# First attention's queries and keys in 256 natural columns, with the mask added by products on TensorE

## What is computed

```python
q = _split_heads(query @ Wq.T + bq)      # query: layernorm(x)
k = _split_heads(key @ Wk.T + bk)        # key, value: the context
v = _split_heads(value @ Wv.T + bv)
scores = jnp.einsum('bhqd,bhkd->bhqk', q, k) / SCALE
scores = jnp.where(attn_mask == 0, jnp.float32(-1000000000.0), scores)
w = jax.nn.softmax(scores, axis=-1)
att = jnp.einsum('bhqk,bhkd->bhqd', w, v)
x = att + key                             # then a layernorm with gamma, beta
```

## Time and profile before

| | us |
|---|---|
| median of three runs | 1006.89 |
| profiled execution | 1014.34 |
| its span, first to last instruction | 1012.5 |
| TensorE busy in the span | 912.5 |
| VectorE busy | 619.8 |
| ScalarE busy | 478.3 |
| GpSimd busy | 351.2 |
| first scores (L576) start | 20.4 |
| last scores (L576) start | 183.3 |

### The profile page before, as it was taken

One profiled execution on the slowest core, in us unless ns is written; L12 is line 12 of the kernel. 1 busy time (PEld: TensorE's weight loads), 2 busy tenths in 40 slices (PEclk: granted clock), 3 DMA queues, 4 the chain that ended last, 5 costly groups with the idle time before them and its releaser, 6 DMA issues. The chain is left out here.

```text
span 1012.5 us, 27004 instructions
## 1 busy us (share of the span) xinstructions
PE 912.5 (90%) x9232; PEld 785.4 (78%) x9233; DVE 619.8 (61%) x1609; ACT 478.3 (47%) x1241; POOL 351.2 (35%) x506
## 2 busy tenths in 40 slices
PE   5899999877999999998999899999999998659996
PEld 4788888637899999986474788888888887547784
DVE  3588888654455555542026556867668668249995
ACT  2878878612222222222344444444444443249894
POOL 1245545430000000007002554555545453246662
PEclk9999999888999999999999989999999999879997
DMA  4454456346811111116854999898897977211221
GB/s 139 143 162 148 151 171 203 121 162 208 298 47 47 47 52 45 48 37 215 308 208 140 170 187 178 147 193 167 175 189 150 203 161 133 47 38 55 63 65 42
DMA packets 220908, 138.34 MB, mean 137 GB/s; under 512 B 159648, under 2 KB 206240, under 8 KB 220704
## 3 DMA queue, kind: packets, MB, share of 16 engines
q1 hardware_dynamic: 173392, 90.86, 36.7%
q10 hardware_dynamic: 44368, 38.08, 13.7%
q0 software_dynamic: 3072, 8.39, 2.7%
HBM read 82.31 MB, written 54.98 MB: 136 GB/s over the span
## 5 line engine op out<-in xcount | busy, mean ns | idle before, releaser
L1604 ACT ACTIVATE c_pT<-c_T 128x512 f32<-128x512 f32 (+2 forms) x90 | 50.2, 595 | 103.6 <-PE c_T L1760 71.8
L1557 POOL TENSOR_TENSOR c_soft<-c_soft,c_share 128x616 f32<-128x616 f32 (+2 forms) x96 | 70.4, 761 | 62.5 <-DVE c_share L2013 60.8
L1027 ACT ACTIVATE b_rowsT<-b_RT 128x256 f32<-128x256 f32 x39 | 15.0, 386 | 161.1 <-PE b_RT L1075 161.1
L1144 DVE COPY b_w<-moe_w 128x1024 f32 x78 | 53.6, 689 | 54.7 <-issue 51.4
L1532 POOL COPY c_pick<-tile_rows 128x2 int32<-128x2 int32 (+1 forms) x16 | 2.9, 179 | 229.7 <-POOLq L934 229.7
L1084 PEld LDWEIGHTS b_G<-b_rowsT,b_w 128*128 128x128 f32 x624 | 77.2, 195 | 4.3 <-DVE b_w L1144 1.5
L1084 PE MATMUL b_G<-b_rowsT,b_w 128*128 128x128 f32 x624 | 77.9, 279 | 1.5 <-ACT b_rowsT L1027 1.3
L1158 DVE SCALAR_TENSOR_TENSOR b_hidT<-b_U,b_bias,b_gate 128x128 f32<-128x128 f32 x156 | 43.9, 344 | 56.6 <-PE b_U L1084 50.4
L1084 PE MATMUL b_U<-b_rowsT,b_w 128*128 128x128 f32 x624 | 76.0, 275 | 0.0
L1111 PE MATMUL b_Y<-moe_w,b_hidT 128*128 x312 | 73.9, 380 | 0.9 <-DVE b_out L1188 0.9
L1084 PEld LDWEIGHTS b_U<-b_rowsT,b_w 128*128 128x128 f32 x624 | 72.8, 192 | 0.0
(11 more groups left out here) (230 smaller groups left out, 2172.3 us busy)
## 6 DMA issues: line engine op xcount, KB each, us to landing
rel_windows<-c_relw ACTq DMA_DIRECT2D x28, 368.0 KB
c_bias<-rel_windows SPq DMA_DIRECT2D x16, 616.0 KB, 5.0
prob_rows<-c_soft SPq DMA_DIRECT2D x16, 616.0 KB
moe_w<-in_L_Wl SPq DMA_DIRECT2D x16, 512.0 KB
values<-c_pT ACTq DMA_DIRECT2D x22, 256.0 KB, 2.6
b_rows<-expert_lists SPq DMA_DIRECT2D x39, 128.0 KB, 2.0
expert_out<-b_out SPq DMA_DIRECT2D x39, 128.0 KB
c_v<-values SPq DMA_DIRECT2D x16, 308.0 KB
```

What stands on the lines that cost most here:

```text
L1144: nc.vector.tensor_copy(own[p][h][:, :, :], w1[:, bass.ds(e, 1), :, h * HE:(h + 1) * HE].rearrange("p o c n -> p (o c) n"))\
L1557: ins = nc.gpsimd.tensor_tensor(soft[p][:, hs, a:z], soft[p][:, hs, a:z], share[:, s, hs].unsqueeze(2).to_broadcast([P, HS, z - a]), ALU.mult)
L1604: nc.scalar.activation(dst, view(T[k]), ACT.Copy, **kw).then_inc(g["emptied"], 1)
```

## The change

The weights of queries and keys keep their 256 columns, two tiles c of 128. A strip of 32 rows now holds two heads. The keys are written twice, kT[:, c, u, :], with the rows of the other head zeroed (keep now has two sides u); one product of a strip's queries (both heads, 32 rows) with both copies (256 columns) gives the scores of both heads. The mask is no longer carried in column 16: four products ahead of the scores, one for each strip, add -1e9 to masked positions. They multiply ones by a tile of 16-bit floats (bf16), masked, whose three nonzero rows hold parts of -1e9 that bf16 holds exactly. keep and masked are computed on GpSimd, three tensor_scalar instructions for each batch, two steps ahead, between std(0) and std(1) of a step; VectorE's keep_mask goes. The wait of load(b + 4) on keep stays as written, though keep is now counted a step later. ScalarE evicts two query tiles instead of four; VectorE writes the keys by two instructions of 256 columns instead of four of 128. In attend the probabilities are picked from other banks (strip, side). As the tiles' addresses shift, two waits for copies out are added in experts.

```diff
@@ layer0, tiles
-        wq = sb("a_wq", [P, KD, MT0 * P])
-        wk = sb("a_wk", [P, KD, MT0 * P])
+        wq = sb("a_wq", [P, KD, D])
+        wk = sb("a_wk", [P, KD, D])
-        keep = [sb(f"a_keep{p}", [P, P]) for p in range(2)]
+        keep = [sb(f"a_keep{p}", [P, 2, P]) for p in range(2)]
+        masked = [sb(f"a_masked{p}", [P, P], BF16) for p in range(2)]
+        ones_b = sb("a_ones", [P, P], BF16)
-        qT = sb("a_qT", [P, MT0, P])
-        kT = sb("a_kT", [P, MT0, P])
+        qT = sb("a_qT", [P, KD, P])
+        kT = sb("a_kT", [P, KD, 2, P])
@@ GpSimd
+            def masks(b, p):
+                if not isinstance(b, int) or b > 1:
+                    apart(pool, g["s_mm"], b - 1)
+                for u in range(2):
+                    nc.gpsimd.tensor_scalar(keep[p][:, u, :], mask_in[p][:, :], 0.0, cst("side")[:, u:u + 1], ALU.is_equal, ALU.is_lt)
+                nc.gpsimd.tensor_scalar(masked[p][:, :], mask_in[p][:, :], 0.0, cst("masked"), ALU.is_equal, ALU.mult)\
+                    .then_inc(g["keep"], 1)
...
-            for b in range(3):
+            for b in range(2):
                 std(0, b)
+                masks(b, b)
+            std(0, 2)
...
             def steps(b, i, p):
                 if there(b + 3):
                     std(0, b + 3)
+                if there(b + 2):
+                    masks(b + 2, p)
                 if there(b - 2):
                     std(1, b - 2)
                     std(2, b - 2)
@@ ScalarE, queries
-                for m in range(MT0):
+                for m in range(KD):
@@ TensorE
-                strips(M[0], wq, [xT[p][:, c, :] for c in range(KD)], range(MT0), g["q_mm"])
+                strips(M[0], wq, [xT[p][:, c, :] for c in range(KD)], range(KD), g["q_mm"])
-                strips(M[1], wk, [cT[p][:, c, :] for c in range(KD)], range(MT0), g["k_mm"])
+                strips(M[1], wk, [cT[p][:, c, :] for c in range(KD)], range(KD), g["k_mm"])
...
-            def scores(b):
+            def scores(b, p):
+                strip = [slice(j * STRIP, (j + 1) * STRIP) for j in range(HPT)]
+                pe.wait_ge(g["keep"], b + 1)
+                since(pe, g["s_exp"], 2 * b)
+                for j, r in enumerate(strip):
+                    nc.tensor.matmul(S[j][:, :, :], ones_b[r, :], masked[p][r, :].unsqueeze(1).to_broadcast([STRIP, MT0, P]),
+                                     start=True, stop=False)
                 pe.wait_ge(g["q_sb"], b + 1)
                 pe.wait_ge(g["k_sb"], b + 1)
-                since(pe, g["s_exp"], 2 * b)
-                for m in range(MT0):
-                    for j in range(HPT):
-                        r = slice(j * STRIP, (j + 1) * STRIP)
-                        ins = nc.tensor.matmul(S[j][:, m, :], qT[r, m, :], kT[r, m, :], start=True, stop=True)
+                for c in range(KD):
+                    for j, r in enumerate(strip):
+                        ins = nc.tensor.matmul(S[j][:, 2 * c:2 * c + 2, :], qT[r, c, :], kT[r, c, :, :], start=False, stop=(c == KD - 1))
                 ins.then_inc(g["s_mm"], 1)
@@ VectorE
-            def keep_mask(b, p):
-                since(dve, g["k_sb"], b - 1)
-                nc.vector.tensor_scalar(keep[p][:, :], mask_in[p][:, :], 0.0, cst("aug"), ALU.not_equal, ALU.not_equal)\
-                    .then_inc(g["keep"], 1)
...
-                for m in range(MT0):
-                    ins = nc.vector.scalar_tensor_tensor(kT[:, m, :], M[1][:, m * P:(m + 1) * P], bk[:, m:m + 1],
-                                                         keep[p][:, :], ALU.add, ALU.mult)
+                for c in range(KD):
+                    ins = nc.vector.scalar_tensor_tensor(kT[:, c, :, :], M[1][:, c * P:(c + 1) * P].unsqueeze(1).to_broadcast([P, 2, P]),
+                                                         bk[:, c:c + 1], keep[p][:, :, :], ALU.add, ALU.mult)
...
-                if front:
-                    keep_mask(b + 3, 1 - p)
@@ experts
+            for out in shared["s_text_out"]:
+                pool.wait_ge(out, 16 * EARLY_HALVES // TEXT_BANKS)
             nc.gpsimd.memset(zeros[:, :], 0.0).then_inc(s_zero, 1)
...
-            dve.wait_ge(shared["s_text_out"][2], 16 * EARLY_HALVES // TEXT_BANKS)
+            for out_copy in shared["s_text_out"][2:]:
+                dve.wait_ge(out_copy, 16 * EARLY_HALVES // TEXT_BANKS)
             combine()
```

More of the change, by code:

```diff
@@ L39 @@
 SCALE0 = 1.0 / DH0 ** 0.5
-MASKED = -1.0e9
+MASKED_PARTS = (-998244352.0, -1753088.0, -2560.0)
+assert sum(MASKED_PARTS) == -1.0e9
 EPS0 = 1e-6
@@ L106, in constants @@
     c["halves"] = np.concatenate([np.eye(P // 2, dtype=np.float32)] * 2)
-    aug = np.zeros((P, 1), np.float32)
-    aug[DH0::STRIP] = 1.0
-    c["aug"] = aug
+    row = np.arange(P)
+    c["side"] = np.stack([row % STRIP // DH0 == u for u in range(2)], axis=1).astype(np.float32)
+    parts = np.zeros((P, 1), np.float32)
+    for n, part in enumerate(MASKED_PARTS):
+        parts[n::STRIP] = part
+    c["masked"] = parts
     e = np.arange(NE, dtype=np.float32)
@@ L161, in layer0 @@
         ident, before, ones = cst("ident"), cst("before"), cst("ones")
-        wq = sb("a_wq", [P, KD, MT0 * P])
-        wk = sb("a_wk", [P, KD, MT0 * P])
+        wq = sb("a_wq", [P, KD, D])
+        wk = sb("a_wk", [P, KD, D])
         wv = sb("a_wv", [P, KD, D])
         wr = sb("a_wr", [P, KD, NE])
-        bq = sb("a_bq", [P, MT0])
-        bqs = sb("a_bqs", [P, MT0])
-        bk = sb("a_bk", [P, MT0])
+        bq = sb("a_bq", [P, KD])
+        bqs = sb("a_bqs", [P, KD])
+        bk = sb("a_bk", [P, KD])
         bv = sb("a_bv", [P, D])
@@ L382, in _ @@
                 nc.gpsimd.memset(va[p][:, :, :], 1.0).then_inc(s_setup, 1)
-            pool.wait_ge(s_setup, 4)
+            nc.gpsimd.memset(ones_b[:, :], 1.0).then_inc(s_setup, 1)
+            pool.wait_ge(s_setup, 5)
+            pool.wait_ge(s_const, 16)
             def inverse_std(link, eps, ready, done, b, k):
@@ L437, in _ @@
             act.wait_ge(s_bqs, 1)
-            act.wait_ge(s_setup, 4)
+            act.wait_ge(s_setup, 5)
             def project(b, p):
@@ L597, in attend @@
                     for k in range(HPT):
+                        strip, side = 2 * (m % 2) + k // 2, 2 * (m // 2) + k % 2
                         ins = nc.tensor.matmul(T[0][k * STRIP:(k + 1) * STRIP, m * P:(m + 1) * P], va[p][:, m * HPT + k, :],
-                                               pT[k][:, m, :], start=True, stop=True, tile_position=(0, k * STRIP))
+                                               pT[strip][:, side, :], start=True, stop=True, tile_position=(0, k * STRIP))
                 ins.then_inc(g["pv_mm"], 1)
@@ L651, in steps @@
                 if there(b):
-                    scores(b)
+                    scores(b, p)
                 if there(b - 1):
@@ L715, in norm_in @@
                 norm_var(norm_stats(b, i, p))
-                keep_mask(b, p)
                 norm_rows(b, p)
@@ L2595, in layout @@
         "x": x, "ctx": ctx_1024, "mask": mask_Bx1x1xS2_ik0.reshape(NB, P),
-        "L0_wqT": strip_columns(L0_xattn_Wq), "L0_wkT": strip_columns(L0_xattn_Wk), "L0_wvT": c(L0_xattn_Wv.T),
+        "L0_wqT": c(L0_xattn_Wq.T), "L0_wkT": c(L0_xattn_Wk.T), "L0_wvT": c(L0_xattn_Wv.T),
         "L0_wrT": c(L0_ffn_Wr.T),
-        "L0_bq": strip_bias(L0_xattn_bq, 1.0 / SCALE0), "L0_bk": strip_bias(L0_xattn_bk, MASKED), "L0_bv": L0_xattn_bv,
+        "L0_bq": L0_xattn_bq.reshape(KD, P).T, "L0_bk": L0_xattn_bk.reshape(KD, P).T, "L0_bv": L0_xattn_bv,
         "L0_gamma": L0_xattn_gamma, "L0_beta": L0_xattn_beta, "L0_br": L0_ffn_br, "L0_pick_bias": L0_ffn_biases_N,
```

9 lines of the change are left out of this document (removed).

## The result

| | before | after |
|---|---|---|
| median of the runs, us | 1007.21 (1006.24 to 1011.64) | 1019.68 (1018.1 to 1020.2) |
| span of the profiled execution, us | 1012.5 | 1017.6 |
| granted clock, mean of the span | 0.967 | 0.954 |
| mean of six loop steps, L765 / L784 to the next, us | 11.34 | 13.06 |

A forecast was written before the change was run, and what follows sets the result against it. The prediction took a ring through GpSimd and VectorE, 10.86 us in a step of 11.55, as the bound, with TensorE's ring close behind. Terms: 1006.89 + 9.6 at full clock + 6.0 for the clock = 1022.5 us; range 1004 to 1036.

The forecast's parts named there:

- the ring: GpSimd scatters, std(0), std(1), VectorE's rows_scaled, keys, list counts, slots, next scatter: 10.86 us, said to hold the loop step.
- M: Time of GpSimd's three mask instructions between std(0) and std(1): 0.70 us each plus 0.05 wait, 2.15 us.
- start and steps up to 3: Start -4.0 us from fewer weights and records; steps 0 and 1 -0.8; steps 2 and 3 +1.8.
- three static steps: The three steps before the loop, where std(1) likewise follows std(0): 3 x 1.4 = +4.2 us.
- six loop steps, full clock: Rolled loop of the first attention: 12.76 us a step instead of 11.34, +8.5 us in all.
- the step after: The step behind the loop, without std(0): 11.4 us instead of 10.46, +0.9.
- last four steps: End of the first attention, where masks have ended: -1.0 us.
- from there to the experts: Stretch between the last attention steps and the experts' first transposes: no term was given.
- clock in the long steps: TensorE's clock halves in idle gaps: 1.5 us a step, expected in 4 of 10 long steps, +6 us.
- rivals D and B: D: price and gains cancel, M near 1.35, 1005 to 1009 us, chance 0.07. B: cheap masks, about 1002, chance 0.13.
- Rival A: Gaps don't bring TensorE's clock down, the ring still costs: 1016.5 us, chance 0.25.
- SyncE: load(b + 4) waits for the masks, leaving some 6 us later in the step: costs nothing, over 3 us to spare.

The follow-up runs named there:

- filling the gap: Changed kernel plus six unused TensorE products ahead of the transposes that wait for the keys, from step 3 on; ratio 1.0082 to the kernel before.
- loads apart: Changed kernel, masks between std(1) and std(2), x's load no longer waiting for keep, mask's load last with its own semaphore; ratio 1.0018 to the kernel before.

## Why the prediction held, and where it didn't

Direction, size and place held: 1022.5 forecast, 1019.68 measured, through the ring that was named. Term by term:

| term | forecast | measured |
|---|---|---|
| one mask set, M | 2.15 | 2.39 |
| start and steps up to 3 | -3.0 | -2.8 |
| three static steps | +4.2 | +4.3 |
| six loop steps, full clock | +8.5 | +10.3 with its falls |
| the step after | +0.9 | +0.8 |
| last four steps | -1.0 | -3.4 |
| from there to the experts | 0 | +2.2 |
| clock in the long steps | +6 | about +2 to +3, within the rows above |
| whole | +15.6 | +12.5 by the medians, 6.8 to 14.0 by the ratio's interval; the rows above sum to +11.4 |

**The ring** is right. Before, its links added to 10.86; with masks they add to 12.92, the three instructions start right behind std(0), and L784 waits 1.66 instead of 0.55. That a cut on TensorE and ScalarE alone would bring at most half a microsecond a step fits the kernel without masks: 11.00 in its loop steps at full clock instead of 11.34, of which VectorE's keys can account for 0.25.

**M** was 0.24 short. Each took 0.74, not 0.70, and the wait and spacing 0.17, not 0.05. The value from the 64- and 256-column rows was near; the cast and the two-input row, which would have left the change level or made it a gain (rivals D and B), were other operations, 2.5 and 1.8 times too cheap. The Trainium skill, "GPSIMD Engine Reference", section 4.1, calls one-input work roughly line-rate. The 0.74 here, beside 0.406 for a two-input product of as many columns, disagrees for this two-operation form. With 2.39 the ring gives 10.86 + 2.39 - 0.25 = 13.00 for a loop step, and 13.06 was measured. Its two steps at full clock took 12.81, so the sum is 0.2 too long, and the falls of the clock add about as much in the mean.

**The clock** is the step that failed, in size. It said "That makes 0.9 to 2.2 a step, 1.5 taken", because "transposes and places (0.41 and about 0.5 us) take twice as long inside the ring", and expected this in 4 of 10 long steps. TensorE's clock did fall, in four of the six loop steps and two of the three static ones, more often than taken. But in three of the four it fell behind the transposes, where it hits scores and probabilities: two of these steps lost nothing that can be told, one some 0.4 by late scores. Only the fourth hit the ring's own products. There the price was 0.99, inside the forecast: 0.52 for transposes and places (the transposes took 0.63 for 0.41, not twice as long) and 0.47 for the late scores. So the number of steps in which the fall reaches the ring was mis-taken more than the price of one. By after's steps at full clock (11.95 static, 12.81 in the loop) the falls of these nine steps are worth 2.8 us; filling the gap gave back 1.85. The Trainium skill, "TensorE: Matmul & The Clock Gate", section "What's actually happening", has activity release the throttled state; that filler products raised the granted clock from 0.89 to 0.96 agrees, and the 1.07 us that it won in the loop show that it is hardly a gain in time where the engine isn't the bound.

That the forecast came within 3 us of the median is partly luck: the 3 to 4 us too much for the clock stand against an M taken 0.24 too short in some twelve places, and the last steps and the way out were off by -2.4 and +2.2. Rival A (1016.5), with M corrected, would have been 1019.4, the time that came, but it has no falls of the clock at all, and there were some. The forecast also took 2.0 us as the least that can be told from no change; the interval of the result is 3.5 us to either side.

**The last steps** gained 3.4 instead of 1.0. There, had shown a stretch at 0.50 in before; and GpSimd waits 1.00, 2.40 and 1.62 us for VectorE ahead of std(1) in three of these steps (L387 in before, 177 to 200 us), so its ring doesn't hold them. That the halved products of queries and keys count there is my reading; no run separates it. I had taken only the absence of masks. **The way out** lost 2.2: the four text products ahead of the last places took 3.58 us in after, 1.96 in before (clock of the window 0.76 and 0.88). This stretch I hadn't costed at all.

**SyncE** was costed at nothing, "with over 3 us to spare", on a landing of 2.6. In after that held: no wait for a load stands among its larger ones, because the ring itself had grown. But the reason was thin: the mask's load freed its reader up to 5.2 us after its issue, and it gates x. The two kernels that moved all three masks later in the step paid for it at once. The start is right: first scores at 16.70 instead of 20.41 (-3.7, forecast -4.0), of which 2.7 are the first queries and keys (3.75 for 6.49) and 0.7 the earlier W_READY. So are the keys (0.88, as taken) and the scores' mask product, hidden in the slack.

## What to carry to other kernels

Before new work goes to the engine with the least work, find the ring that closes over several engines and put the work into that engine's waiting time outside it: the same three instructions cost 21 us ahead of std(1) and about 10 less one place later. Then follow every transfer that waits on a counter moved with them; here one such load cost 2.7% behind the masks on VectorE. And a count of instructions in the ring is worth more than the engines' busy time: two of three could be left out, which with their place made the loss a gain, while 6.7 us less work on TensorE in the loop made next to none. Last, read a step's length beside its granted clock: in one kernel a fall lies in slack, in the next it costs a microsecond a step.

## What the runs showed of the hardware

- tensor_scalar on GpSimd, 128 columns, two operations, a column scalar, int32 in: 0.74 us, to f32 and bf16 alike; a two-input product of as many columns 0.406.
- Beside GpSimd's masks VectorE's rows_scaled took 0.61 instead of 0.48 us, in the kernel with masks between std(1) and std(2) and loads apart. With three masks there rows_out, behind it, averages 0.57, with one mask 0.48 as before: order and number on GpSimd also set which of VectorE's instructions run beside it.
- A granted clock of 0.89 instead of 0.96 over the loop cost 1.1 us of 78 with the masks ahead of std(1); without masks a step at 0.86 took 12.0 us, one at full clock 11.0.
- A 64 KB load, 3.0 us from issue to landing in the median of that run, freed its reader after 5.2 us in one step.
- One first indirect scatter stood 5.3 us with no releaser in the profile: not explained.
